# A Mamba-type mixer, attention and experts on one core: copies, a diagonal sum, tap order, gate steps and set-up moved between engines

## The reference

```python
x = x + _L0_attn_a_ref(_layernorm(x), ...)   # state mixer, 32 heads of 64, state 128
x = x + _L0_ffn_ref(_layernorm(x), ...)      # attention of 16 heads + 8 experts (layer 0)
x = x + _L0_attn_b_ref(_layernorm(x), ...)   # gated sum of 9 rolled copies
x = x + _L0_ffn_ref(_layernorm(x), ...)      # the same attention + experts (layer 1)

# state mixer: the parts that the change touches
xBC = silu(sum((xp[:, i:i + T, :] * conv_w[:, i] for i in range(K))))   # K = 4 taps
dt, lam = softplus(dt + dt_bias), softplus(L * dl)
qk = einsum('btgn,bsgn->bgts', Cm, Bm)
att = qk * decay * lam_ts          # lam_ts picks one of 15 levels by (t, s)
y = einsum('bhts,bshp->bthp', att, v) + x * D
# attention of layers 0 and 1
probs = softmax(einsum('bqhd,bkhd->bhqk', q, k) * scale)
out = einsum('bhqk,bkhd->bqhd', probs, v)
```

## Time and profile before

| | us |
|---|---|
| median of 3 runs | 2415.45 |
| lowest, highest | 2414.69, 2421.06 |
| the profiled execution | 2413.47 |
| its span, first to last instruction | 2411.6 |
| PE busy in the span | 2117.2 |
| DVE busy | 1880.2 |
| ACT busy | 1411.4 |
| POOL busy | 825.8 |

### The profile page before, as it was taken

One profiled execution on the slowest core, in us unless ns is written; L12 is line 12 of the kernel. 1 busy time (PEld: TensorE's weight loads), 2 busy tenths in 40 slices (PEclk: granted clock), 3 DMA queues, 4 the chain that ended last, 5 costly groups with the idle time before them and its releaser, 6 DMA issues.

```text
span 2411.6 us, 47467 instructions
## 1 busy us (share of the span) xinstructions
PE 2117.2 (88%) x16768; PEld 1603.1 (66%) x16768; DVE 1880.2 (78%) x4629; ACT 1411.4 (59%) x2980; POOL 825.8 (34%) x1188
## 2 busy tenths in 40 slices
PE   2768889998999899998989999898989999898866
PEld 1546657676777677676767767677767767676544
DVE  7776878788897878788887878888787878865433
ACT  1545556666575766656576666657576665654323
POOL 5111343424333342424333342433334242424131
PEclk9989999999999999999999999999999999998868
DMA  4020212120111212110211212011121211011110
GB/s 144 6 48 6 52 41 50 43 47 19 43 42 41 55 41 50 36 38 29 47 48 41 51 44 46 20 40 45 41 54 41 50 36 38 26 41 45 40 40 5
DMA packets 255194, 100.58 MB, mean 42 GB/s; under 512 B 118552, under 2 KB 253856, under 8 KB 254400
## 3 DMA queue, kind: packets, MB, share of 16 engines
q1 hardware_dynamic: 254960, 97.55, 15.6%
HBM read 51.12 MB, written 46.14 MB: 40 GB/s over the span
## 4 chain that ended last, share of the span: by engine, by line
PE 55%; DVE 27%; issue 6%; POOL 5%; ACT 4%; DMA 2%; SPq 0%; DVEq 0%; POOLq 0%; ACTq 0%
PE psB L810 9%; PE psB L800 8%; DVE work L1132 7%; PE psA L581 5%; PE psB L741 5%; DVE nmax L1212 5%; PE psA L641 4%; DVE att L1164 3%; PE psA L666 3%; PE psA L617 2%; PE psB L726 2%; PE psA L621 2%; POOL O_sb L1417 2%; PE psA L634 2%; PE psB L688 1%
## 5 line engine op out<-in xcount | busy, mean ns | idle before, releaser
L1132 DVE SCALAR_TENSOR_TENSOR work<-psA,c_conv_w,work 128x255 f32<-128x255 f32 (+2 forms) x864 | 401.8, 479 | 42.7 <-ACT work L884 21.6
L581 PE MATMUL psA<-xnT_a,c_w_in 128*128 128x256 f32 x1088 | 310.9, 406 | 37.8 <-DVE work L1132 33.8
L1212 DVE TENSOR_REDUCE nmax<-psB 128x2 f32<-128x512 f32 x512 | 315.5, 677 | 28.0 <-PE psB L708 28.0
L957 ACT ACTIVATE pt<-psB 128x512 f32<-128x512 f32 x512 | 264.3, 603 | 63.8 <-PE psB L727 63.6
L800 PE MATMUL psB<-x1T,c_w 128*128 128x256 f32 x1024 | 275.7, 394 | 21.2 <-ACT hid L999 19.6
L810 PE MATMUL psB<-c_w,hid 128*128 128x128 f32 x2048 | 269.5, 279 | 1.5 <-ACT hid L980 0.8
L810 PEld LDWEIGHTS psB<-c_w,hid 128*128 128x128 f32 x2048 | 259.8, 195 | 15.3 <-issue 5.0
L911 ACT ACTIVATE att<-psA 128x512 f32<-128x512 f32 x384 | 207.5, 604 | 103.6 <-PE psA L617 59.8
L1164 DVE TENSOR_TENSOR att<-att,QK 128x1024 f32<-128x1024 f32 x192 | 253.1, 1352 | 6.0 <-ACT att L911 5.7
L581 PEld LDWEIGHTS psA<-xnT_a,c_w_in 128*128 128x128 f32 x1088 | 197.3, 200 | 85.9 <-DVE work L1132 52.0
L980 ACT ACTIVATE hid<-psB,c_b 128x256 f32<-128x256 f32 x512 | 215.4, 479 | 66.5 <-PE psB L800 51.6
(11 more groups left out here) (234 smaller groups left out, 4309.9 us busy)
## 6 DMA issues: line engine op xcount, KB each, us to landing
qk_scr<-qparts SPq DMA_DIRECT2D x192, 192.0 KB, 2.3
q_stack<-qk_scr SPq DMA_DIRECT2D x32, 576.0 KB
k_stack<-qk_scr SPq DMA_DIRECT2D x32, 576.0 KB
lvl_scr<-work SPq DMA_DIRECT2D x32, 192.0 KB, 5.4
low<-lvl_scr SPq DMA_DIRECT2D x256, 1.5 KB
c_w_in<-in_in_wT SPq DMA_DIRECT2D x1, 2176.0 KB, 8.5
x<-in_x SPq DMA_DIRECT2D x16, 128.0 KB, 2.2
c_w<-in_W SPq DMA_DIRECT2D x2, 1024.0 KB
```

The costliest lines, as they stand in the source:

```text
L581: e.matmul(t[:, 0:T], w_in[:, first + j * P:first + (j + 1) * P], xnT_a[:, :], start=True, stop=True).then_inc(filled[b], 1)
L957: e.activation(pt_b[a % PTS][:, :, :].rearrange("p h q -> p (h q)"), t[:, :], ACT.Exp, scale=float(AD) ** -0.5).then_inc(drained[b], 1)
L1132: m = e.scalar_tensor_tensor(out=cv[:, back:], in0=t[:, 0:T - back], scalar=conv_w[:, c, tap:tap + 1], in1=cv[:, back:], op0=ALU.mult, op1 ...
L1212: e.tensor_reduce(nmax[:, i, 2 * h2:2 * h2 + 2], t[:, :].rearrange("p (h k) -> p h k", k=T), AX.X, ALU.max).then_inc(drained[b], 1)
```

## The change

1. The eight copies of attention's sums to `O_sb` (4 per layer) move from DVE (`ep`, L1223) to ACT, in new hops `ocopy`, with their own places in the list.
2. The diagonal of C.B: POOL multiplies B and C elementwise into `bc_prod` (new hop `bcp`), PE multiplies it by a column of ones in two matmuls of one column into the same bank as `qk`, after a wait for POOL; ACT copies all 386 columns (`qkc`), and DVE keeps only the coefficient (`coef`).
3. `taps` does tap by tap over both tiles in turn, each instruction waiting for its own tile's last one.
4. Two steps of the gates (`W2t`, and the floor of `CL`) are written as scalar_tensor_tensor with both operands the same tile, in place of tensor_scalar.
5. `tail0` takes both reciprocals first, then both products.
6. POOL's set-up of sample 0: four blocks of `low` in hop gates5, the other four, the stacks and `V9` behind the level parts in gates6. `lvl_scale` is loaded into a part of `X`.
7. A new list `PERIOD`. It begins at another point of the same cycle, so lags are one higher for most hops and run up to 5.

The list, one line of each (start of before, start of after):

```diff
-load_x0.0+0 zgate0.7+1 zact0.6+1 zact0.7+1 up1.2+4 maxt0.0+2 mix1.12+3 qk0.0+1 down1.1+4 own0.0+1 relu1.2+4
...
+load_x0.0+0 es0.3+3 ocopy0.2+3 weigh0.4+2 own0.3+2 exps0.3+3 down1.4+5 own0.4+2 wexp0.4+2 gated0.2+2 prod0.4+2
```

The rest of the diff, cut:

```diff
@@ tensor, qk @@
+                    e.wait_ge(bc_product, n + 1)
+                    for i in range(NT):
+                        m = e.matmul(t[:, 3 * P + i:3 * P + i + 1], bc_prod[:, i * P:(i + 1) * P], ones_f[:, 0:1],
+                                     start=True, stop=True, skip_group_check=True)
                     m.then_inc(filled[b], 1)
@@ scalar @@
+                elif what == "qkc":
+                    t, b, u = bank(("qk", 0, n, 0))
+                    e.wait_ge(filled[b], u + 1)
+                    e.activation(QK_all[:, :], t[:, 0:3 * P + NT], ACT.Copy).then_inc(drained[b], 1)
+                elif what == "ocopy":
+                    t, b, u = bank(("ep", lay, n, k))
+                    e.wait_ge(filled[b], u + 1)
+                    e.activation(O_sb[:, k, :], t[:, 0:T], ACT.Copy).then_inc(drained[b], 1)
@@ vector, gates @@
-                    e.tensor_scalar(W2t[:, :, :], W1t[:, :, :], 1.0, None, ALU.add).then_inc(w_ready, 1)
+                    e.scalar_tensor_tensor(out=W2t[:, :, :], in0=W1t[:, :, :], scalar=1.0, in1=W1t[:, :, :],
+                                           op0=ALU.add, op1=ALU.max).then_inc(w_ready, 1)
...
-                    e.tensor_scalar(CL[:, :, :, :].rearrange("p i l h -> p i (l h)"), SPL[:, :, 2 * H:], 1e-37, None,
-                                    ALU.max).then_inc(cl_in, 1)
+                    e.scalar_tensor_tensor(out=CL[:, :, :, :].rearrange("p i l h -> p i (l h)"), in0=SPL[:, :, 2 * H:], scalar=1e-37,
+                                           in1=SPL[:, :, 2 * H:], op0=ALU.max, op1=ALU.max).then_inc(cl_in, 1)
@@ vector, taps @@
-                    for j, c in enumerate(conv_tiles(k)):
-                        e.wait_ge(tap_done, tap_count(n, c))
-                        for back in range(1, KCONV):
-                            tap = KCONV - 1 - back
+                    done = [0, 0]
+                    for back in range(1, KCONV):
+                        tap = KCONV - 1 - back
+                        for j, c in enumerate(conv_tiles(k)):
+                            if back == 1:
+                                e.wait_ge(tap_done, tap_count(n, c))
+                            else:
+                                e.wait_ge(dve_step, done[j])
                             m = e.scalar_tensor_tensor(out=cv[:, back:], in0=t[:, 0:T - back], scalar=conv_w[:, c, tap:tap + 1],
                                                        in1=cv[:, back:], op0=ALU.mult, op1=ALU.add)
@@ vector, qk becomes coef; ep is gone @@
-                    e.tensor_copy(QK[:, :, :].rearrange("p k t -> p (k t)"), t[:, 0:3 * P]).then_inc(drained[b], 1)
-                    e.wait_ge(*empty(hop))
-                    for i in range(NT):
-                        e.tensor_tensor(qk_scr[:, :], QK[:, i, :], ident[:, :], ALU.mult).then_inc(*own.step())
-                        e.wait_ge(*own.now())
-                        e.tensor_reduce(qk_diag[:, i:i + 1], qk_scr[:, :], AX.X, ALU.add).then_inc(*own.step())
-                        e.wait_ge(*own.now())
+                elif what == "coef":
+                    e.wait_ge(*empty(("qk", 0, n, 0)))
...
-                elif what == "ep":
-                    e.tensor_copy(O_sb[:, k, :], t[:, 0:T]).then_inc(drained[b], 1)
@@ gpsimd @@
+                elif what == "gates" and k == 5 and n == 0:
+                    e.wait_ge(dve_setup, 1)
+                    for q in range(NQ):
+                        e.tensor_copy(low_buf[0:QT, q * QT:(q + 1) * QT, :], bc(ident[0:QT, 0:QT], 2, H)).then_inc(*own.step())
+                elif what == "bcp":
+                    e.wait_ge(silu_done, silu_count(n, -1))
+                    e.tensor_tensor(bc_prod[:, :], bmT, cmT, ALU.mult).then_inc(bc_product, 1)
```

More of the change, by code:

```diff
@@ L305, in build @@
         O_sb = sb("O_sb", [P, 4, T])
-        rden = sb("rden", [P, NH])
+        rden = sb("rden", [P, NT, NH])
         attnT = sb("attnT", [P, T])
@@ L1227, in _ @@
                         e.wait_ge(ff_taken, ends_ahead[hop])
+                    heads = [bank(hop, qt)[0][:, :].rearrange("p (h c) -> p h c", c=32) for qt in range(NT)]
                     for qt in range(NT):
[L1229 to L1235 removed]
+                        e.wait_ge(*full(hop, qt))
+                        e.reciprocal(rden[:, qt, :], heads[qt][:, :, AD]).then_inc(*own.step())
+                    for qt in range(NT):
+                        e.wait_ge(dve_step, own.n - NT + 1 + qt)
+                        e.tensor_tensor(o_tok[:, qt, :].rearrange("p (h c) -> p h c", c=AD), heads[qt][:, :, 0:AD],
+                                        bc(rden[:, qt, :], 2, AD), ALU.mult).then_inc(drained[bank(hop, qt)[1]], 1)
+                    for qt in range(NT):
                         e.wait_ge(*empty(hop, qt))
@@ L1376, in _ @@
                     e.tensor_tensor(c_parts[:, :, 2, :], cr, c_parts[:, :, 1, :], ALU.subtract).then_inc(c_ready, 1)
+                    if n == 0:
+                        for q in range(NQ, T // QT):
+                            e.tensor_copy(low_buf[0:QT, q * QT:(q + 1) * QT, :], bc(ident[0:QT, 0:QT], 2, H)).then_inc(
+                                *(own.step() if q < T // QT - 1 else (pool_setup, 1)))
+                        e.memset(q_stack[:, :, :], 0.0).then_inc(*own.step())
+                        e.memset(k_stack[:, :, :], 0.0).then_inc(*own.step())
+                        e.wait_ge(*own.now())
+                        e.memset(k_stack[64:SLOTROWS, :, :], 1.0).then_inc(*own.step())
+                        e.wait_ge(*own.now())
+                        e.memset(V9[:, :, :, :], 0.0).then_inc(*own.step())
+                        e.wait_ge(*own.now())
+                        e.memset(V9[:, :, :, AD:AD + 1], 1.0).then_inc(pool_setup, 1)
                 elif what == "q":
```

104 lines of the change are left out of this document (41 added, 63 removed).

## The result

| | before | after |
|---|---|---|
| median, us | 2416.46 (4 runs, 2414.69 to 2421.06) | 2361.87 (4 runs, 2359.91 to 2366.18) |
| span of the profiled execution | 2411.6 | 2360.1 |
| start of the program to the first mark | 135.7 | 138.8 |
| three filling turns | 371.1 | 363.4 |
| one full turn | 137.53 | 133.03 |

The ratio is 0.9774, with a 95% interval of 0.9754 to 0.9793: 2.3% faster. The forecast was 2353 us, with a range of 2317 to 2397. A mark here is the start of the last record of a sample's one-column mean-of-squares matmul, which follows the second weight product; it counts sixteen samples in either kernel. The twelve full turns won 53.9 us, the filling turns 7.7, the start lost 3.1 and the end 7.0; together 51.5 us of span.

A forecast was written before the change was run, and what follows sets the result against it. PE was taken to set the pace, DVE in places, with 10.0 us of PE idle time a turn to win. Full turns 42.6, filling turns 6, start 8.3, first convolution 3.5: 2413.5 - 60.4 = 2353 us, range 2317 to 2397.

The forecast's parts named there:

- The full turn: Each of twelve full turns: shorter PE waits, less new PE work and new waits, win 3.55 us, 42.6 in all.
- (a): PE reaches a step whose input is just being made, nothing ready between: 2.45 us a turn, 2.1 to be won.
- (d): PE's remaining waits in smaller pieces: 4.3 us a turn, 1.4 to be won by lighter DVE and filled gaps.
- The taps: DVE's convolution taps over two tiles in turn: 0.3 us a pair, 2.7 a turn, bounds 0 and 3.6.
- (b): PE's waits on DVE's queue in the convolution and gated-sum stretch: 2.4 us a turn, 1.2 to be won.
- Rival 4: DVE's taps in turn save nothing, by the rule on its pipe: 2368 us, chance 0.08.
- The copies: Eight O_sb copies of 0.422 us moved from DVE to ACT: DVE loses 3.4 us a turn.
- Rival 3: ACT's O_sb copies come late behind its queue and PE waits, 0.8 us a copy: 2430 us, chance 0.07.
- Rival 1: PE's waits only move, old gaps close and others open; a full turn wins 0.5 us: 2394 us, chance 0.21.
- Rival 2: PE's waits nearly vanish, a full turn wins 6.4 us: 2316 us, chance 0.12.
- The start: Set-up of sample 0: first tap at 42.7 instead of 51.06, 8.3 us won; first sample's convolution, 3.5 us won.
- The end: Drain after the sixteenth sample, same steps in nearly the same order: nothing, between -3 and +3 us.

The follow-up runs named there:

- list_alone: New list with the code of before (only the loading of lvl_scale into X kept), against the kernel before: 2501.4 us, ratio 1.0353.
- taps_undone: Changed kernel with each tile's three taps in a row again: 2414.7 us, ratio 0.9991 to the kernel before, full turn 136.31 us.
- code_alone: Kernel before with all code edits but the old list, each new hop right behind its origin: 2450.9 us, ratio 1.0146 to before.
- code_osb_dve: As code_alone, old list and changed code, but the O_sb copies given back to DVE: 2417.0 us, ratio 1.0001 to the kernel before.
- gates_undone: Changed kernel with both gate steps as tensor_scalar again: 2355.6 us, ratio 0.9739 to the kernel before.
- fills_undone: Changed kernel with POOL's set-up back in its old place, all ahead of the level parts: 2364.5 us, ratio 0.9781 to the kernel before.
- fills_late: Changed kernel with POOL's fills of the stacks and V9 moved behind bc_prod of sample 0: 2355.0 us, ratio 0.9745 to before.

## Why the prediction was right, and where it was not

**The full turn**, 3.55 us forecast, 4.50 measured: the largest term, right in size, and the working behind it is half wrong. The bound held: PE's idle time was what could be won, and 4.2 of 10.0 us went. DVE's sum came out as forecast, 107.0 for 108; ACT 90.3 for 91; PE 127.2 for 128.3. But I priced the new list by the waits of kind (a) and (d), 3.5 us that it would win by filling PE's gaps. By list_alone it loses 5.5 us a turn unless DVE is lighter, 3.7 of them in PE's busy time at a lower clock, which my sum took as fixed. I took DVE's 22 us of idle time a turn as room. A part of it, 6.4 us in front of the copies, was time in which the queue stood still, and the new list leaves less of the rest between DVE and PE.

**The taps**, 0.3 us a pair forecast, 0.52 measured; 4.7 us a turn is also above my bound of 3.6. I let four inner steps be worth 0.075 each, and took 0.44 us as the free pace, from a pair of records with their tails in it (0.88 for two). From start to start it is 0.39, as 2.42 us for six with a record of 0.47 shows. The term was mis-sized by 2.0 (2.7 against 4.7), and its worth to the turn by more: I let it count a third through kind (b), it counts 3.3 us. Rival 4, which followed from the rule on DVE's pipe (the Trainium skill, VectorE: DVE Perf Modes, "The DRAIN you can't avoid"), is refuted by this row and by taps_undone: the next instruction starts 0.08 us before the last record ends when nothing holds it. The same section adds that a next operation that is not held starts earlier, which I had left out; this row agrees with that sentence.

**The copies.** I counted 3.4 us of DVE. What they were worth is 4.3 us of turn, since DVE's standing in front of them went too; the earlier trace rows showed this idle time (12.8 us before 16 copies), and I read it only as a sign that DVE was always ready. Rival 3 had the right mechanism for the wrong engine and place: at the old places of the list ACT stands 8.6 us a turn in front of its copies, and that costs 2.7 us a turn (code_alone against code_osb_dve). At the new list's places it stands 1.8 us.

**The diagonal**: 1.5 us of DVE and the reductions forecast, 1.4 us of turn measured with PE's two matmuls paid. **The gate steps**: a cost of 0.3 us on DVE forecast, 0.6 measured (gates_undone), the far one of my bounds; the turn did not change by it.

**Rival 1** (the waits only move) is true of the list by itself and worse, and false of the whole. **Rival 2** would have needed 6.4 us a turn.

**Filling turns**: 6 forecast, 7.7 measured.

**The start**, 8.3 and 3.5 forecast won, 3.1 measured lost: a miss of 15 us. By my own sign, a first tap later than 49 us, this part of the prediction is wrong: it came at 50.8. The step that failed is "I put the end of this set-up at 41 to 42": it ended at 49.2. From `high_sel` to `ident_bf` it took 16.2 us beside POOL's casts and fills, and 5.8 without the fills. I took the casts as the only ones to be held, at up to 3.5 us each; one of `high_sel` took 5.49, and I left out the small steps on `conv_edge`, of which one took 3.42 us for a work of 0.18. My lower bound of 2 us was not low enough either, as the first tap came only 0.25 us earlier. That is 8 of the 15 us. The other 7 lie between the first tap and the first mark: I gave 3.5 us won, and 3.4 were lost (88.0 us for 84.6). Here the lower level of PE's clock held longer. Each projection took at least 0.63 us until 78.3 us after the change and 0.38 from 78.8 on; in the kernel before the same step came between 64.0 and 65.8 us. The last weight products (9.16 us for 64, first fence) cost another 1.5, with the clock at 0.50 from 126.5 to 133.3 us. In fills_undone, whose code behind the set-up is that of the changed kernel, eight projections at 64.75 us already take 1.99 us together, where eight at 63.51 us after the change take 3.78, and the stretch is 84.1 us. So the loss goes with the clock and not with the new code; what sets when the clock rises isn't shown.

**The end**, 0 forecast, 7.0 measured lost, outside my 3. It differs between kernels that are alike there, from 261.5 (after) to 266.3 (gates_undone), so some 5 us of it follow how the engines happen to fall; the old list has 254.5 and 254.7, but 258.1 and 261.8 with the new code, and the new list with the old code has 265.9. PE is busy for 185.4 us of it after and for 188.4 before, so what grew is PE's idle time. The granted clock over the whole stretch is nearly the same, 0.81 after and 0.82 before. What of it is the change is left open.

The two misses, 15 us at the start and 7 at the end, met 11 us and 2 won beyond the forecast in the turns, which left the time 9 us above. So the total came out close in part by luck: errors of 22 us one way met 13 the other.

## What to carry to other kernels

An order of work and the weight of the engines under it are one change: the new list here is 3.5% slower with the old code, and two parts of the code, the taps and the copies, each carry the whole gain or more. The bottleneck's own busy time is not fixed either: with a list that makes PE wait more, the same matmuls took 3.7 us a turn longer at a lower granted clock. Time in which an in-order engine stands at an instruction whose input isn't ready is not slack; everything behind it is held, so a copy that moves to another engine should also get its place behind the end of what it reads (argued from the waits, not run by itself). And a part's price belongs to the list that it was measured in: the same edit of the taps gave 0.5 us a turn in one and 3.3 in the other.

Set-up work on POOL costs DVE's casts whole fills when they run side by side. Moved to where DVE has steps that read PSUM, it won 7 us in the median, and with the casts on ACT 13.5, of which only the first part was traced to its cause.

## What the runs showed of the hardware

- DVE's independent three-operand steps of 255 columns, reading PSUM, start 0.39 us apart while each record lasts 0.47 (2.42 us for six); dependent ones 0.49.
- A DVE step on 18 columns of SBUF with one input takes 0.18 us alone and took 3.42 beside a fill. The cast of 128 columns (third of `high_sel`) began beside a cast of `low`, which ended at 38.6, and was then held through the fill behind it, until 42.1:

```profile
36.65 5.49 DVE L1119 CAST high_sel<-Z 128x128 bf16<-128x128 f32 x1
```

The 4.52 us of the `conv_edge` step in the fence on the start lie within that cast's record, so they are this hold and not one of its own: a long record behind a held instruction isn't a second hold. A step with two SBUF inputs was not held beside a fill at all; in fills_late the edge correction takes 0.17 us beside `q_stack`, and the taps, which read PSUM, 2.42:

```profile
45.78 2.42 DVE L1152 SCALAR_TENSOR_TENSOR work<-psA,c_conv_w,work 128x255 f32<-128x255 f32 x6
...
47.10 3.51 POOL L1371 MEMSET q_stack<- 96x4096 bf16 x1
...
48.31 0.17 DVE L1162 TENSOR_TENSOR work<-work,conv_edge 128x6 f32<-128x6 f32 x1
```

That is what the Trainium skill, SBUF — State Buffer, section "🔬 SBUF: two separate sides", states: a two-input instruction is excluded only by a GpSimd one that reads SBUF. One-input casts and steps beside fills were held, more of them than I had counted, and one for 5.5 us where I had taken 3.5 from a row.
- A printed clock of 1.00 at the start of a program can be an empty row. The stretch from 50 to 65 us after the change is given as 1.00, yet its projections take 0.63 us each. The trace's clock records begin only at 78.7 us there and at 65.0 in the kernel before, which is where the projections change from 0.63 to 0.38 us. The same step shows around a later stretch of the kernel before, for which there is a record of the lower level: four of the projections in it take 0.63 us and start 0.43 us apart, those behind it take 0.38 and start 0.22 apart:

```profile
75.30:78.70 3.40, 2.75 (x9) 2.39 (x10) 2.81 (x7) 1.43 (x4) 0.00 (x0) 0.50 0.20 59
```

```profile
76.86 2.36 PE L581 MATMUL psA<-xnT_a,c_w_in 128*128 128x256 f32 x6
...
80.53 1.03 PE L581 MATMUL psA<-xnT_a,c_w_in 128*128 128x256 f32 x4
```

A sum for a first sample should take its durations from rows of the first sample.
- With the list of list_alone the clock falls to the lower level (1.2 GHz) twice in each full turn, for 3.4 or 6.8 us each time, while PE is busy 92% of the turn.
